# Causal attention with a three-product output projection whose weights are split one stage earlier and streamed per head, and joined fronts of four stages

## The reference

```python
x = x + L0_xattn(ln(x), ctx, ...)   # 16 heads of 16, int8-rounded query and output products
x = x + L0_ffn(ln(x), ...)          # product-key lookup, 4 heads, 8 rows each
x = x + L1_xattn(ln(x), ctx, ...)   # linear attention with a gate
x = x + L1_ffn(ln(x), ...)          # 4-bit weights:
    w_up = ((w_up_q - 7.5) * repeat(w_up_scale, 64, axis=1)).T
    y1 = x1 @ w_up + b_up + x1 @ w_up_lora_a @ w_up_lora_b     # 1024 hidden units, rank 16
    x2 = relu(y1)
    y2 = x2 @ w_down + b_down + x2 @ w_down_lora_a @ w_down_lora_b
x = x + L2_xattn(ln(x), ctx, ...)   # one-head attention over the context
x = x + L2_ffn(ln(x), ...)          # a whole block:
    h = rmsnorm(x, ln1_w)
    q, k, v = h @ wq, h @ wk, h @ wv                           # 16 heads of 128
    attn = softmax(where(causal, q @ k.T / sqrt(128), -1e9))   # per sequence and head
    x = x + (attn @ v) @ wo                                    # wo: 2048 x 256
    h = rmsnorm(x, ln2_w); 16 gated experts, the best 6 per token, and a shared one
x = x + L3_xattn(ln(x), ctx, ...)   # 16 heads of 16, gated
x = x + L3_ffn(ln(x), ...)          # 16 gated experts, the best 2 per token:
    scores = softmax(xf @ gate_w.T); topk_w, topk_idx = top_k(scores, 2)
```

## Time and profile before

| | |
|---|---|
| runs, us | 4588.35, 4598.83, 4601.52; median 4598.83 |
| profiled execution, us | 4605.66 |
| its span, us | 4603.9, mean granted TensorE clock 0.936 |
| first products of ffn4, mha, us | 1472.65, 1803.34 |
| stage starts, us | lin 1204, ffn4 1424.6, mem 1701.9, mha 1786.4, moe2a 2861, att32 3863.7, moe3 4241.7 |

### The profile page before, as it was taken

One profiled execution on the slowest core, in us unless ns is written; L12 is line 12 of the kernel. 1 busy time (PEld: TensorE's weight loads), 2 busy tenths in 40 slices (PEclk: granted clock), 3 DMA queues, 4 the chain that ended last, 5 costly groups with the idle time before them and its releaser, 6 DMA issues. The chain is left out here.

```text
span 4603.9 us, 74464 instructions
## 1 busy us (share of the span) xinstructions
PE 4047.8 (88%) x25328; PEld 3353.4 (73%) x25328; DVE 2595.6 (56%) x5873; ACT 2070.3 (45%) x5341; POOL 903.5 (20%) x738
## 2 busy tenths in 40 slices
PE   6885999999896877999999997999979998887791
PEld 4554899999774765877877886788868886665671
DVE  6887989899474337444444443433333333776533
ACT  6884666666222433433433333433333333675140
POOL 1112333233000430000000000222222222001245
PEclk8997999999997997999999998999989998998595
DMA  2001000000001003000000001100010000001244
GB/s 67 14 15 44 1 0 0 0 0 1 28 21 42 0 30 115 6 6 6 6 6 6 6 5 34 34 10 9 5 54 10 9 10 24 12 12 42 84 135 127
DMA packets 100309, 119.50 MB, mean 26 GB/s; under 512 B 13792, under 2 KB 81216, under 8 KB 99776
## 3 DMA queue, kind: packets, MB, share of 16 engines
q1 hardware_dynamic: 93168, 97.25, 6.6%
q0 software_dynamic: 6864, 18.75, 1.5%
HBM read 93.03 MB, written 22.94 MB: 25 GB/s over the span
## 5 line engine op out<-in xcount | busy, mean ns | idle before, releaser
L1191 ACT ACTIVATE peer_tab<-peer_sims 128x128 f32<-128x128 f32 x1024 | 305.7, 393 | 0.0
L1198 POOL TENSOR_TENSOR peer_tab<-peer_sims 128x2048 f32<-128x2048 f32 x64 | 246.3, 3868 | 289.3 <-ACT peer_sims L1175 260.1
L1246 DVE SCALAR_TENSOR_TENSOR peer_tab<-peer_tab,peer_th 128x2048 f32<-128x2048 f32 x128 | 298.2, 2371 | 2.6 <-ACT peer_tab L1191 2.3
L1263 PE MATMUL bank<-ident,peer_tab 128*128 128x128 f32 x2048 | 247.9, 275 | 24.6 <-DVE peer_tab L1246 24.6
L1263 PEld LDWEIGHTS bank<-ident,peer_tab 128*128 128x128 f32 x2048 | 234.5, 142 | 37.9 <-DVE peer_tab L1246 25.4
L1673 DVE COPY mha_ks<-bank 128x512 f32<-128x512 f32 x128 | 88.4, 691 | 302.5 <-PE bank L1638 300.1
L1778 PE MATMUL bank<-mha_wo,mha_oT 128*128 128x256 f32 x1024 | 243.6, 381 | 0.0
L1313 PE MATMUL bank<-peer_wd,peer_hh 128*128 128x256 f32 x1024 | 242.0, 379 | 1.2 <-DVE peer_hh L1304 1.2
L1286 PE MATMUL bank<-peer_hT,peer_wg 128*128 128x256 f32 x1024 | 242.7, 380 | 0.0
L668 DVE TENSOR_TENSOR moe2a_b<-moe2a_a,bank 128x512 f32<-128x512 f32 x104 | 71.4, 687 | 270.9 <-PE bank L576 239.8
L1286 PEld LDWEIGHTS bank<-peer_hT,peer_wg 128*128 128x128 f32 x1024 | 195.2, 191 | 26.6
(11 more groups left out here) (533 smaller groups left out, 11101.1 us busy)
## 6 DMA issues: line engine op xcount, KB each, us to landing
m_y_rows<-moe_y SPq DMA_DIRECT2D x79, 128.0 KB, 1.7
att_ctxT<-in_ctxT_dram SPq DMA_DIRECT2D x32, 256.0 KB, 2.7
lin_ctxT<-in_ctxT_dram SPq DMA_DIRECT2D x16, 256.0 KB, 2.8
mem_ctxT<-in_ctxT_dram SPq DMA_DIRECT2D x16, 256.0 KB, 2.8
mem_ctx<-in_ctx_dram SPq DMA_DIRECT2D x16, 256.0 KB, 3.1
t_scratch<-mha_hTf SPq DMA_DIRECT2D x8, 512.0 KB, 4.6
moe2a_hTf<-t_scratch SPq DMA_DIRECT2D x8, 512.0 KB, 3.7
moe2b_hTf<-t_scratch SPq DMA_DIRECT2D x8, 512.0 KB, 3.7
```

Of the source, the lines that this page charges most:

```text
L1191: i = nc.scalar.activation(tab[g][h][:, b * P:(b + 1) * P], sims[:, g, h, P:2 * P], ACT.Identity, bias=sims[:, g, h, b:b + 1])
L1198: nc.gpsimd.tensor_tensor(out=tab[g][h][:].rearrange("p (a b) -> p a b", b=P), in0=sims[:, g, h, P:2 * P].unsqueeze(1).broadcast_to([P, NB ...
L1246: nc.vector.scalar_tensor_tensor(out=tab[g][h][:], in0=tab[g][h][:], scalar=th[:, g, h:h + 1], in1=tab[g][h][:], op0=ALU.is_ge, op1=ALU.mu ...
L1263: i = nc.tensor.matmul(TB[n % 2][:, j * P:(j + 1) * P], tab[g][h][:, blk * P:(blk + 1) * P], core.ident[:], start=(j == 0 and h == 0), sto ...
```

## The change

- **Output projection.** `oT` becomes a pair `oTs` (hi on ACT, lo on DVE by the new `applied_low_dve`, run three steps behind), `wo` becomes a pair per head, and `out_pe` does three fp32r products where it did one float32 product: twelve a head. `apply_pe` and `out_pe` wait for the low part.
- **Its weights.** `wo` is loaded and split in the memory stage (`round_out_act` on ACT, `low_out_pool` on POOL, in eight pieces, one a unit) and written to DRAM as `mha_wo` (4 MB) before that stage ends. The attention stage loads 256 KB of it per head into four buffers, in every tile (`load_out_sp`), and `tail_sp` moves into that sequence.
- **Loads a stage ahead.** `AttentionInputs` holds the first four raw pieces, the norm weights and the mask, loaded at the end of the memory stage; `DequantInputs` holds the 4-bit stage's inputs, loaded at the end of the linear attention stage.
- **4-bit front.** `dequant_block` is gone; its work is in the stage's own block, in an order that has the norm between the scaling and the sums, five banks for the rank-16 products, and a semaphore per part.
- **att8 and att32.** The fills of `vbd` move behind the first norm on POOL, and DVE waits only for `fixed`.
- **moe3.** The routing chain runs over the first six tiles once their logits are there, and then over the last two.

```diff
-def dequant_block(core, st, wgs, wds, bup, bdn, NB):
...
-            pe.wait_ge(q_in, 16 * len(loads))
-            for n, (rows, cols, target) in enumerate(parts):
-                if n >= 4:
-                    pe.wait_ge(added, n - 3)
-                width = cols.shape[-1]
-                nc.tensor.matmul(bank[n % 4][:, 0:width], rows, cols, start=True, stop=True).then_inc(lora, 1)
...
-            dve.wait_ge(q_in, 16 * len(loads))
-            nc.vector.scalar_tensor_tensor(out=wg[:], in0=gq[:], scalar=7.5, in1=gs[:], op0=ALU.subtract, op1=ALU.mult)
-            nc.vector.scalar_tensor_tensor(out=wd[:], in0=dq[:], scalar=7.5, in1=ds[:], op0=ALU.subtract,
-                                           op1=ALU.mult).then_inc(scaled, 1)
-            dve.wait_ge(scaled, 1)
-            for n, (rows, cols, target) in enumerate(parts):
-                dve.wait_ge(lora, n + 1)
-                width = cols.shape[-1]
-                nc.vector.tensor_tensor(out=target, in0=bank[n % 4][:, 0:width], in1=target, op=ALU.add).then_inc(added, 1)
-            for n, (w, parts_) in enumerate(((wg, wgs), (wd, wds))):
-                dve.wait_ge(hi_made, n + 1)
-                nc.vector.tensor_tensor(out=parts_[1][:], in0=w[:], in1=parts_[0][:], op=ALU.subtract)
...
-            act.wait_ge(added, len(parts))
-            nc.scalar.activation(wgs[0][:], wg[:], ACT.Copy).then_inc(hi_made, 1)
-            nc.scalar.activation(wds[0][:], wd[:], ACT.Copy).then_inc(hi_made, 1)
...
+class DequantInputs(Stage):
...
+    def load_sp(self, sp):
+        for out, in_ in self.up:
+            sp.dma_start(out, in_).then_inc(self.up_in, 16)
+        for out, in_ in self.small:
+            sp.dma_start(out, in_).then_inc(self.small_in, 16)
+        for out, in_ in self.down:
+            sp.dma_start(out, in_).then_inc(self.down_in, 16)
...
+        LB = bank[2:7]
...
+            if relu and is_first(t):
+                pe.wait_ge(down_lo_made, 1)
...
+    def lora_pe(pe, parts, first_part):
+        for n, (rows, cols, target) in enumerate(parts, first_part):
+            if n >= len(LB):
+                pe.wait_ge(added, n - len(LB) + 1)
+            nc.tensor.matmul(LB[n % len(LB)][:, 0:cols.shape[-1]], rows, cols, start=True, stop=True).then_inc(lora, 1)
+
+    def scale_dve(dve, w, q, scale, arrived, count):
+        dve.wait_ge(arrived, count)
+        nc.vector.scalar_tensor_tensor(out=w[:], in0=q[:], scalar=7.5, in1=scale[:], op0=ALU.subtract, op1=ALU.mult).then_inc(scaled, 1)
+
+    def add_lora_dve(dve, parts, first_part, n_scaled):
+        dve.wait_ge(scaled, n_scaled)
+        for n, (rows, cols, target) in enumerate(parts, first_part):
+            dve.wait_ge(lora, n + 1)
+            nc.vector.tensor_tensor(out=target, in0=LB[n % len(LB)][:, 0:cols.shape[-1]], in1=target, op=ALU.add).then_inc(added, 1)
+
+    def round_act(act, w, parts, n_added, made):
+        act.wait_ge(added, n_added)
+        nc.scalar.activation(parts[0][:], w[:], ACT.Copy).then_inc(made, 1)
+
+    def low_part_dve(dve, w, parts, hi_made, made):
+        dve.wait_ge(hi_made, 1)
+        nc.vector.tensor_tensor(out=parts[1][:], in0=w[:], in1=parts[0][:], op=ALU.subtract).then_inc(made, 1)
...
+                pe.wait_ge(inputs.small_in, inputs.n_small)
+                lora_pe(pe, lora_up, 0)
             for j in range(NB):
                 front_pe(pe, 0, j)
                 if peer:
                     pre_pe(pe, 1, 1, j)
+            if relu:
+                lora_pe(pe, lora_down, N_UP)
+                pe.wait_ge(up_lo_made, 1)
...
+                    round_act(act, wg, wgs, N_UP, up_hi_made)
+                    round_act(act, wd, wds, N_LORA, down_hi_made)
...
+                    scale_dve(dve, wg, inputs.gq, inputs.gs, inputs.up_in, inputs.n_up)
+                    front_dve(dve, 0, 0, NORM)
+                    add_lora_dve(dve, lora_up, 0, 1)
+                    scale_dve(dve, wd, inputs.dq, inputs.ds, inputs.down_in, inputs.n_down)
+                    front_dve(dve, 0, 0, LOW)
+                    low_part_dve(dve, wg, wgs, up_hi_made, up_lo_made)
+                    add_lora_dve(dve, lora_down, N_UP, 2)
+                    low_part_dve(dve, wd, wds, down_hi_made, down_lo_made)
...
+class AttentionInputs(Stage):
...
+    def load_sp(self, sp):
+        for k, (n, c) in enumerate(self.first):
+            sp.dma_start(self.raw[:, k, :], self.core.args[n][c * P:(c + 1) * P, 0:512]).then_inc(self.raw_in[k], 16)
+        for out, in_ in self.norms:
+            sp.dma_start(out, in_).then_inc(self.norms_in, 16)
...
-    wo = sb("wo", [P, NH, D])
-    ln1, ln2, causal = sb("ln1", [P, C]), sb("ln2", [P, C]), sb("causal", [P, S])
+    WOR = 4
+    wo = [sb(f"wo{i}", [P, 2, D], FP32R) for i in range(WOR)]
...
-            pe.wait_ge(oT_ready, n)
+            pe.wait_ge(oT_low, n)
...
+    def applied_low_dve(dve, t, s):
+        dve.wait_ge(oT_ready, t * NH + s + 1)
+        for pair in range(2):
+            half = slice(2 * pair * P, 2 * (pair + 1) * P)
+            hi, lo = (part[:, s % 2, half].rearrange("p (g b q) -> p b g q", b=2, q=S) for part in oTs)
+            i = nc.vector.tensor_tensor(out=lo, in0=O[:, half].rearrange("p (b g q) -> p b g q", b=2, q=S), in1=hi, op=ALU.subtract)
+        i.then_inc(oT_low, 1)
+
+    def load_out_sp(sp, t, s):
+        n = t * NH + s
+        if some(n - WOR + 1):
+            sp.wait_ge(out_done, n - WOR + 1)
+        sp.dma_start(wo[s % WOR][:].rearrange("p k d -> p (k d)").bitcast(FP32), wo_rows[:, s * 2 * D:(s + 1) * 2 * D]).then_inc(wo_in[s % WOR], 16)
+
     def out_pe(pe, t, s):
         n = t * NH + s
-        pe.wait_ge(oT_ready, n + 1)
+        pe.wait_ge(oT_low, n + 1)
+        pe.wait_ge(wo_in[s % WOR], (t * (NH // WOR) + s // WOR + 1) * 16)
         if s == 0:
-            if isinstance(t, int) and t == 0:
-                pe.wait_ge(wo_in, 16)
             if some(t):
                 pe.wait_ge(y_used, t)
         for g in range(GT):
-            i = nc.tensor.matmul(Y[g // 2][:, (g % 2) * D:(g % 2 + 1) * D], oT[:, s % 2, g * P:(g + 1) * P], wo[:, s, :],
-                                 start=(s == 0 and g % 2 == 0), stop=(s == NH - 1), skip_group_check=True)
+            for m, (ph, pw) in enumerate(((0, 0), (0, 1), (1, 0))):
+                i = nc.tensor.matmul(Y[g // 2][:, (g % 2) * D:(g % 2 + 1) * D], oTs[ph][:, s % 2, g * P:(g + 1) * P], wo[s % WOR][:, pw, :],
+                                     start=(s == 0 and g % 2 == 0 and m == 0), stop=(s == NH - 1 and m == 2), skip_group_check=True)
         i.then_inc(out_done, 1)
...
+        after(t, s, 3, applied_low_dve, dve)
...
+            if not inputs_loaded:
+                inputs.load_sp(sp)
             load_quad_sp(sp, 0, slice(RAWS, None))
+            for s in range(WOR):
+                load_out_sp(sp, 0, s)
             load_quad_sp(sp, 1)
-            sp.dma_start(wo[:], args["a_wo"].rearrange("(n p) d -> p n d", p=P)).then_inc(wo_in, 16)
-            for quad in range(2, NH // QUAD):
-                load_quad_sp(sp, quad)
-            tail_sp(sp, 0)
-            with sp.Fori(1, NT) as t:
-                tail_sp(sp, t)
+            load_quad_sp(sp, 2)
+            load_out_sp(sp, 0, 4)
+            load_quad_sp(sp, 3, slice(0, RAWS))
+            for s in range(5, 9):
+                load_out_sp(sp, 0, s)
+            load_quad_sp(sp, 3, slice(RAWS, None))
+            for s in range(9, NH):
+                load_out_sp(sp, 0, s)
+
+            def tile_sp(t):
+                for s in range(NH):
+                    load_out_sp(sp, t, s)
+                    if s == TAIL + 1:
+                        tail_sp(sp, t - 1)
+
+            with sp.Fori(1, NT - 1) as t:
+                tile_sp(t)
+            tile_sp(NT - 1)
+            tail_sp(sp, NT - 1)
...
+            for l in (3, 2, 1):
+                applied_low_dve(dve, NT - 1, NH - l)
...
+    def blank_values_pool(pool):
+        nc.gpsimd.memset(vbd[0][:], 0.0).then_inc(zeroed, 1)
+        nc.gpsimd.memset(vbd[1][:], 0.0).then_inc(zeroed, 1)
+        pool.wait_ge(zeroed, 2)
+        for i in range(2):
+            for j in range(2):
+                m = nc.gpsimd.memset(vbd[i][64 * j:64 * j + 64, :, :, j, HD:HV], 1.0)
+            m.then_inc(zeroed, 1)
+        pool.wait_ge(zeroed, 4)
+
     def unit_gp(pool, t, par):
         if exists(t + 2):
             norm_pool(pool, t + 2)
+        if is_int(t, -2):
+            blank_values_pool(pool)
...
-            dve.wait_ge(zeroed, 3)
+            dve.wait_ge(fixed_set, 1)
...
+                ahead.load_sp(sp)
...
+        NHD, FIRST = 16, 4
+        wo_raw, wo_parts = sb("wo_raw", [P, NHD, D]), sb("wo_parts", [P, NHD, 2, D], FP32R)
+        wo_in, wo_hi, wo_lo, wo_stored = (sem(n) for n in ("wo_in", "wo_hi", "wo_lo", "wo_stored"))
+
+    def round_out_act(act, n):
+        act.wait_ge(wo_in, 16)
```

(34 more changed lines are left out.)

214 lines of the change are left out of this document (112 added, 102 removed).

## The result

The changed kernel takes 4553.15 us (median of 4, 4552.06 to 4553.52) against 4598.67; the ratio is 0.9905 (95% interval 0.9887 to 0.9922), so 45.5 us less. The forecast was 4550. In a second series it took 4548.58 (ratio 0.9885, 0.9869 to 0.9902), so differences of less than some 5 us between medians of two series say nothing. Its profiled execution took 4553.52 us, with a span of 4551.8.

| stage | before | after | difference | forecast |
|---|---|---|---|---|
| att8 | 371.3 | 368.1 | -3.1 | -2.8 |
| peer | 831.6 | 831.6 | 0 | 0 |
| lin and ffn4 | 499.1 | 471.6 | -27.4 | -28, +0.9 for a closing block |
| mem | 84.5 | 87.0 | +2.5 | +2 |
| mha | 1075.0 | 1059.1 | -15.8 | -17.8, +0.9 |

What follows compares the result with a forecast made beforehand. TensorE, busy 88% of the span, was taken as the bound, with each edit costed in its own stage. The terms summed to -49 us: 4557 from the profiled 4605.66, 4550 against the median 4598.83; range 4530 to 4577 (8 in 10).

Steps and rivals of the forecast that it cites:

- closing block: Two more closing blocks for the early buffers, each like the 0.86 us gap before a norm: +1.7 us together.
- the likeliest case: Whole kernel: the forecast itself, 4538 to 4562 us, given 55%.
- Products: Attention's output projection: twelve one-pass products for four full-precision ones, 0.265 us saved in each of 128 head steps, -34 us.
- The source: Rows 4, the expert stage's down projection: the same twelve products in 1.44 us, 0.12 each, taken as the price.
- the prediction's other bound: Output projection: products at half of the 512-wide ones, 12 x 0.115 = 1.38 us a head, -41 us.
- The rival of the loads: Output projection, each head: weight loads bind the products, +74 for -34, total +59, 4658 us; chance 3%.
- Tails: Attention tile tails: VectorE's new subtraction delays the tail and the copy of K; 0.98 x 7 = +7 us.
- The first tile's stall: Attention's first tile: fourth quad's last pieces queue behind head 8's load; +5.7 wait, +1.5 half clock, +7.2 us (0 to +10).
- The start: Start of attention: four piece loads (1 MB) go ahead of the second quad's, +1.5 us (0 to 4).
- The memory stage: Splitting the output weights there: the 4 MB write that SP awaits may show, +2 us (0 to +9).
- The 4-bit stage: Its front: first product at 1443.5 instead of 1472.65, second tile's norm costs about 1.3; -28 us (-22 to -32).
- Routing: Last stage: vector chain over six tiles early, then the last two; ends 4298.6 instead of 4302.29, -3.6 us (-6 to 0).

Runs made afterwards that it cites:

- The full-precision run: Changed kernel with the output projection again four full-precision products a head, high parts alone: 4583.23 us, ratio 0.9964 to the kernel before.
- The reordering: Changed kernel with the fourth quad's last two pieces ahead of head 8's output weights in SyncE's queue: 4544.03 us, ratio 0.9877 to the kernel before.
- the two second executions: Changed kernel and kernel before, each run once more with nothing edited: 4548.58 us and 4598.89 us.

## Why the prediction was right, step by step

The time lies in the range, and the likeliest case came in. That it lies so near, within 4 us, is in part luck: in the attention stage two terms of together +7 that the sum did not have met 7 us more of gain from the products.

- **Products.** 0.32 us a step and not 0.265: -41 instead of -34. The source, held (1.49 against 1.44), with 0.07 of it the change to fp32r. What the sum left out is what surrounds the projection: against a step without one, the next step's first group falls from 0.55 to 0.47 and the product with v from 0.84 to 0.82, so the projection adds 1.39 (7.42 less 6.03), not 1.44. The 0.32 equals the prediction's other bound (-41), which was worked out from another price, so that is chance. The full-precision run gives the same 0.31 the other way. The rival of the loads fell: four more loads a step, and the step is shorter, its products 0.12 us apart. By the Trainium skill's rule (TensorE: Matmul & The Clock Gate, Part 3, What overlaps and what doesn't) these loads, all on the same rows, could not have overlapped; the traces do not agree (loads recorded at 0.19 us behind products 0.12 us apart). One figure in that rival was wrong: it put the point where the whole change comes to nothing at 0.18 us a product, but by its own sum (1.70 us now, -15 for the rest) that point is near 0.15 (0.12 us more a head, 12 x 0.151 = 1.82: +15 - 15).
- **Tails.** The wait for the copy of k grew from 0.87 (0.70 in the last tile) to 1.90, as written down: +7.4 for +7. The size was right; of its parts the shorter steps weigh a little more and the subtraction a little less (above).
- **The first tile's stall.** 5.58 us for 5.7, the pieces issued 8.0 us into the ninth step for 8.0, and 1.6 of half clock behind it for 1.5. The reordering removed that, 7.3 us of the first tile.
- **The start.** +0.3 at the first product, +1.1 at the sixth step, where a wait of 0.90 us for ScalarE's copy of q has come. Without the new subtraction on VectorE 0.5 us of it goes, so that is its part; the rest is not traced. +1.5 was forecast, at another place.
- **Not in the sum.** The loop's head: five waits that sum to 9.2 us, 5.2 before, +4.0. And half-clock spells: two between the first tile and the drain, +3.2. These are two missing terms of the attention stage, and the larger gain of the products hid them. The measured terms are -41 + 7.4 + 7.2 + 1.4 + 4.0 + 3.2 = -18, against -15.8 for the stage; the drain, which gave 0.2 and not the 1.3 of its four projections, explains 1 of the 2. The other is open.
- **The memory stage.** +2.5 for +2 (+3.7 between the two second executions); the 4 MB land in 13.5 us, where the prediction took 11 to 12.
- **The 4-bit stage.** -27.4 for -27.1 net, first product 18.85 us in for 19.0.
- **The rest.** att8 -3.1 for -2.8. att32 shows no gain (+0.7, with 2.5 us between two traces of the kernel before). Routing -3.6 for -3.6; the other 5 us of the last stage are the first execution's of the kernel before.

## What to carry to other kernels

Where an engine is full, cost an edit by the distance between the same instruction in two successive steps, the change of precision included. Shorter steps on one engine bring the others' backlogs forward: of the 41 us of products some 14 came back as waits that had been there, smaller, before, and as half clock behind them (7.4, 4.0 and 3.2; 2 to 3 of the 7.4 are the new subtraction's). A load that waits for later work belongs behind every load that earlier work needs, in the same queue.

## What the runs showed of the hardware

- **The clock falls behind some waits of nearly 2 us.** In twelve traces of the attention stage (the changed kernel and its variants), TensorE ran 3 to 4 us at 1.2 GHz (granted clock 0.5) behind the first tile's wait of 5.6 to 6.1 us in each of the ten that have it, and behind six of the seven waits of 2.94 us, with about 1.6 us lost each time (the drain, where TensorE stands idle more, is left out). Behind 77 waits of 1.75 to 2.05 us it did so 16 times: three times in three of the traces, never in four others that have such waits. Behind 48 waits of 1.2 to 1.7 us it never did. By that a wait of 1.9 us can cost 3.5 (an estimate, 1.9 and 1.6).
- **A loop's head costs what the queued work does not cover.** Instructions are fetched at each jump back, and the body's first product comes 2.55 to 3.16 us after that transfer starts (70 loop heads). The wait that is left is 0.8 to 1.2 us behind four full-precision products, 1.4 to 2.1 behind twelve short ones, 1.1 to 1.4 with one head's four long ones among short ones.
- **Weight loads of 128 columns, recorded at 0.19 us, stand behind products spaced 0.12 us**, twelve of each in 1.49 us. The stage has 512 more of them than before, and its steps are shorter.
